# Layer 1's first eight blocks of edge records, loaded by SyncE during the node stage

## The reference

```
# layer 0: per edge a tensor product of x[dst] with 32 edge attributes, summed by src
tp = fctp_messages(x[dst], edge_attr_32, W1, W2, W3, W4)
agg = segment_sum(tp @ Wm + bm, src)
x = layernorm(x + x + concat(x, agg) @ Wu + bu)
# layer 1: per edge a radial weight from 10 lengths, times y[src] and 4 edge attributes, summed by dst
w = relu(edge_attr_10 @ W_fc1 / sqrt(10)) * sqrt(2) @ W_fc2 / sqrt(100)
y = linear(x) * a            # W_l1_0, W_l1_1
s = segment_sum(products of w, y[src], edge_attr_4, dst) / 4
x = layernorm(x + self(x) * a + 0.5 * linear(s) * a)
```

## Time and profile before

| | |
|---|---|
| median of three runs | 2830.84 us |
| the profiled execution's own time | 2835.33 us |
| its span | 2833.5 us |
| TensorE busy (matmul) | 2614.8 us, 92% |
| VectorE | 1979.4 us, 70% |
| ScalarE | 852.2 us, 30% |
| GpSimd | 1662.2 us, 59% |
| granted TensorE clock, mean | 0.977 |

### The profile page before, as it was taken

One profiled execution on the slowest core, in us unless ns is written; L12 is line 12 of the kernel. 1 busy time (PEld: TensorE's weight loads), 2 busy tenths in 40 slices (PEclk: granted clock), 3 DMA queues, 4 the chain that ended last, 5 costly groups with the idle time before them and its releaser, 6 DMA issues. The chain is left out here.

```text
span 2833.5 us, 54044 instructions
## 1 busy us (share of the span) xinstructions
PE 2614.8 (92%) x16778; PEld 2330.6 (82%) x16778; DVE 1979.4 (70%) x5259; ACT 852.2 (30%) x2319; POOL 1662.2 (59%) x1770
## 2 busy tenths in 40 slices
PE   4999999999999999996999968999999999998997
PEld 2888788888888888886999958988888888888886
DVE  7677567766667767663777856766777676667766
ACT  2444344444444444431222212222222222222221
POOL 1666566666666666662100017777777777777775
PEclk8999999999999999998999979999999999999999
DMA  6899999999888999865888845333333333333332
GB/s 232 294 314 314 299 319 316 319 324 320 290 290 287 291 300 294 294 215 187 279 279 280 284 141 149 90 86 88 100 86 90 86 101 88 86 88 99 87 88 68
DMA packets 433880, 584.01 MB, mean 206 GB/s; under 512 B 75752, under 2 KB 372409, under 8 KB 421002
## 3 DMA queue, kind: packets, MB, share of 16 engines
q10 hardware_dynamic: 237795, 282.85, 30.4%
q0 software_dynamic: 84144, 149.09, 17.9%
q1 hardware_dynamic: 111656, 148.48, 16.3%
HBM read 352.08 MB, written 228.11 MB: 205 GB/s over the span
## 5 line engine op out<-in xcount | busy, mean ns | idle before, releaser
L444 POOL DMA_INDIRECT placed<-message,slots_now x784 | 762.9, 973 | 486.5 <-ACT message L613 326.6
L1429 POOL DMA_INDIRECT f_y<-y_table,b_rec x894 | 855.4, 957 | 289.6 <-issue 181.9
L528 PEld LDWEIGHTS g_bank<-quad_ring,front_work 128*128 128x128 f32 x6272 | 878.5, 191 | 98.9 <-issue 96.5
L528 PE MATMUL g_bank<-quad_ring,front_work 128*128 x6272 | 942.1, 304 | 8.0 <-DMA quad_ring<-products 7.5
L772 DVE SCALAR_TENSOR_TENSOR front_work<-g_bank,quarter_node,front_work 128x512 f32<-128x512 f32 x784 | 529.6, 743 | 44.2 <-PE g_bank L505 31.8
L1619 PE MATMUL e_bank<-f_msg,f_hot 128*126 128x160 f32 x1788 | 387.6, 312 | 71.7 <-DVE f_msg L1493 70.6
L1490 DVE TENSOR_TENSOR f_msg<-e_bank,f_y 128x256 f32<-128x256 f32 x447 | 189.2, 423 | 319.7 <-issue 223.9
L1614 PE MATMUL e_bank<-f_msg,f_hot 128*126 128x160 f32 x1788 | 395.8, 303 | 18.0 <-DVE f_msg L1493 15.3
L1619 PEld LDWEIGHTS e_bank<-f_msg,f_hot 128*126 128x126 f32 x1788 | 282.0, 189 | 122.9 <-DVE f_msg L1493 121.4
L1602 PE MATMUL e_bank<-fc,b_hidden 100*128 100x192 f32 x1788 | 372.0, 330 | 0.0
L613 ACT COPY message<-g_bank 128x320 f32<-128x320 f32 x392 | 167.2, 427 | 561.9 <-PE g_bank L528 561.9
(11 more groups left out here) (237 smaller groups left out, 2622.7 us busy)
## 6 DMA issues: line engine op xcount, KB each, us to landing
products<-g ACTq DMA_DIRECT2D x49, 2560.0 KB
quad_ring<-products ACTq DMA_DIRECT2D x98, 1280.0 KB
big<-placed SPq DMA_DIRECT2D x49, 1458.0 KB, 7.1
front_work<-in_e_t SPq DMA_DIRECT2D x392, 64.0 KB
b_lengths<-length_parts ACTq DMA_DIRECT2D x447, 45.0 KB
placed<-zeros SPq DMA_DIRECT2D x24, 648.0 KB
f_y<-y_table,b_rec POOLq DMA_INDIRECT x894
placed<-message,slots_now POOLq DMA_INDIRECT x784
```

The lines of the kernel that those rows point to most:

```text
L444: pool.indirect_dma_start(v.placed[:, :], bass.IndirectOffsetOnAxis(slots_now[tile // SET % SLOT_SETS][:, tile % SET:tile % SET + 1], 0), ...
L528: last = pe.matmul(bank_now[:, n * D:n * D + D], spread[batch % SPREADS][:, j, q * P:q * P + P], ring[:, bass.ds(slot + j, 1), :].rearrang ...
L1429: pool.indirect_dma_start(f_y[:, tile % Y_RING, :], None, v.y_table[:, :], bass.IndirectOffsetOnAxis(b_rec[b % REC_RING][:, j, 0:1], 0)).t ...
```

## The change

The tiles `b_rec` are allocated before the node stage and live on. In the fast form of the node stage, SyncE's list gets a fifth entry, last in each step: at steps 24 to 31 it loads the register and issues the records of one of the first eight blocks. One semaphore, `first_records`, counts all eight. In layer 1 these loads are gone; GpSimd and VectorE wait for `first_records` at block 0 and for the tile's own semaphore from block 8 on. The semaphore `excess_ready` is gone: what it counted is counted on `misfit_ready`, and TensorE waits for 2 there.

```diff
+        v.b_rec = [sb(f"b_rec{q}", [P, TPB, 6], I32) for q in range(REC_RING)]
+        v.first_records = sem("first_records")
...
-                pe.wait_ge(excess_ready, 1)
-                pe.wait_ge(misfit_ready, 1)
+                pe.wait_ge(misfit_ready, 2)
...
+        RECORDS_FROM = 24
...
-                (unrolled if fast else skewed)(sp, FAST_BLOCKS, N, (7 if fast else 4, load_rows), (5 if fast else 4, load), (1, store), (0, landed))
+                def load_records(b):
+                    first = sp.value_load(v.block_start[b:b + 1, :], min_val=0, max_val=TILES * P)
+                    edges = t["records"][bass.ds(first, BLOCK_EDGES), :]
+                    sp.dma_start(v.b_rec[b][:].rearrange("p j a -> p (j a)"), edges.rearrange("(p j) a -> p (j a)", p=P)).then_inc(v.first_records, 16)
+
+                def some_records(i, k):
+                    b = i * N + k - RECORDS_FROM
+                    if 0 <= b < REC_RING:
+                        load_records(b)
...
+                unrolled(sp, FAST_BLOCKS, N, (7, load_rows), (5, load), (1, store), (0, landed), (0, some_records))
...
-                    if b >= REC_RING:
-                        sp.wait_ge(weighed, (b - REC_RING + 1) * BPP)
+                    sp.wait_ge(weighed, (b - REC_RING + 1) * BPP)
...
-                for b in range(REC_RING):
-                    load_block(b // SUBS, b % SUBS)
...
-                        pool.wait_ge(rec_in[b % REC_RING], 16 * (b // REC_RING) + 16)
+                        if b == 0:
+                            pool.wait_ge(v.first_records, 16 * REC_RING)
+                        if b >= REC_RING:
+                            pool.wait_ge(rec_in[b % REC_RING], 16 * (b // REC_RING))
```

More of the change, by code:

```diff
@@ L44 @@
 SLOTS = ROWS * P
+REC_RING = 8
 LEAST = 14 * P
@@ L283, in front_phase @@
         tiles_counted, nodes_in, start_ready = sem("tiles_counted"), sem("nodes_in"), sem("start_ready")
-        excess_ready, misfit_ready, held_summed, violations_summed = sem("excess_ready"), sem("misfit_ready"), sem("held_summed"), sem("violations_summed")
+        misfit_ready, held_summed, violations_summed = sem("misfit_ready"), sem("held_summed"), sem("violations_summed")
         features_doubled = sem("features_doubled")
@@ L692, in block_starts @@
                     tables.link(dve.tensor_tensor(excess[:], starts[:, 2:4], starts[:, 0:2], ALU.subtract))
-                    dve.tensor_scalar(excess[:], excess[:], float(BLOCK_EDGES), 0.0, ALU.subtract, ALU.max).then_inc(excess_ready, 1)
+                    dve.tensor_scalar(excess[:], excess[:], float(BLOCK_EDGES), 0.0, ALU.subtract, ALU.max).then_inc(misfit_ready, 1)
                 def weights():
@@ L946, in landed @@
                     sp.sem_inc(stored, 1)
-                (unrolled if fast else skewed)(sp, FAST_BLOCKS, N, (7 if fast else 4, load_rows), (5 if fast else 4, load), (1, store), (0, landed))
+                def load_records(b):
[6 more added lines that the diff above has]
+                        load_records(b)
+                if not fast:
+                    for b in range(REC_RING):
+                        load_records(b)
+                    skewed(sp, FAST_BLOCKS, N, (4, load_rows), (4, load), (1, store), (0, landed))
+                    return
+                unrolled(sp, FAST_BLOCKS, N, (7, load_rows), (5, load), (1, store), (0, landed), (0, some_records))
             def fast_sync(sp):
@@ L1286, in layer1_edges @@
         HIDDEN_RING = 3
-        REC_RING = 8
         COLUMNS = 4
-        b_rec = [v.sb(f"b_rec{q}", [P, TPB, 6], I32, local) for q in range(REC_RING)]
+        b_rec = v.b_rec
         b_column = [v.sb(f"b_column{q}", [P, TPB], F32, local) for q in range(COLUMNS)]
@@ L1465, in localise @@
                 def localise(b):
-                    dve.wait_ge(rec_in[b % REC_RING], 16 * (b // REC_RING) + 16)
+                    if b == 0:
+                        dve.wait_ge(v.first_records, 16 * REC_RING)
+                    if b >= REC_RING:
+                        dve.wait_ge(rec_in[b % REC_RING], 16 * (b // REC_RING))
                     dve.tensor_scalar(b_column[b % COLUMNS][:], b_rec[b % REC_RING][:, :, 1], v.block_base[:, b:b + 1], None, ALU.subtract).then_inc(columns, 1)
```

## The result

The changed kernel takes 2837.04 us (median of 17 runs, 2831.18 to 2843.23) against 2830.84 for the kernel before (17 runs, 2824.16 to 2836.99): ratio 1.0022, 95% interval 1.0014 to 1.003. In a second comparison it was 1.0013 (1.0004 to 1.0022). It is slower by about 0.2%, and the predicted 2834.8 was 2.2 us too low.

What follows compares the result with a forecast made beforehand. POOL's gathers bound layer 1; PE and a loop through SP, level, bound the node stage. Node stage +3.6 and layer 1 +0.4 gave +4.0 us, a median of 2834.8 against 2830.84; range 2829.0 to 2840.0.

Steps and rivals of the forecast that it cites:

- The bound: Layer 1 bound by POOL's gathers; node stage by PE and a loop through SP, level, so added delay has no cover.
- (a): Node stage, steps 24 to 31: each record load delays SP's placed rows by 1.45 us; stage +3.6 us.
- 0.8 of 2.0 us of unevenness: Node stage: 2.0 us of the eight steps measured before was unevenness; a longer loop keeps less than half, adding 0.8.
- The landing on an emptier queue: Node stage: placed rows issued later land sooner, in 6.85 us instead of the median 7.1.
- The register load: Node stage: SP's register load from DRAM stays near the quiet figure, 0.45 to 0.66 us, between two placed-row loads.
- (b): Layer 1 opening: POOL can gather 2.6 us earlier, but only about 1.1 is free before it waits for pair 8's weighing.
- (c): Layer 1 opening: own-table copy starts eleven us earlier beside ACT's first loads; pair 8 weighed 1.6 us later, layer +0.4.
- The upper bound of +2.6: Layer 1: worst case if ACT's register loads cost 2.25 us and nothing is regained; 4.7 - 1.1 = 3.6, rounded down.
- A: Node stage: SP's register loads slow, 1.2 us more each; +8.4 there and +0.4, 2839.6 us; chance 0.16.
- B: Node stage: the queue, not the issue, is the limit; stage pays 0.2, POOL keeps 1.1 to 2.6; 2829.2 us; chance 0.15.
- C: Layer 1 opening: loads beside the copy cost 2.6, plus node stage 3.6; +6.2, 2837.0 us; chance 0.10.
- D: Layer 1: POOL is not released earlier because it is late itself; worth 0 on top of the forecast; chance 0.04.

Runs made afterwards that it cites:

- second comparison: The changed kernel, unaltered, run again on another chip against the kernel before: 2843.57 us, ratio 1.0013.
- the reordering: Changed kernel with the eight record loads moved ahead of SyncE's wait for the finished block: 2837.97 us, 0.9994 of the kernel before; 0.9985 on a slower chip.
- the dose: Two thrown-away register loads a step in 32 node-stage steps, added to Copy at 1: 2854.0 us (1.0063) behind the store, 2838.69 (1.0013) ahead of the wait.
- Copy at 1: The reordering, plus layer 1's copy of the own table held until one pair is weighed: 2835.01 us (0.998 of the kernel before); other chips 0.9986 and 1.0.
- at 7: The reordering, plus layer 1's copy of the own table held until seven pairs are weighed: 2837.74 us, 0.9991 of the kernel before; 0.9984 on a slower chip.
- the version at the tail: Copy at 1 with records behind the store at steps 42 to 45, two blocks each, after the last placed-rows load: 2831.84 us, 0.9989 of the kernel before.

## Why the prediction was right or wrong

**The bound.** Right. Layer 1's end follows the gathers: from pair 16's gather to the last one it is 1086.13 us before and 1084.91 after. The node stage has no cover for SP's delay, as the reordering (5.6 us in the whole time for nothing but a place, 2.7 of them in the node stage of the profiles) and the dose (16.3 us in the node stage) show.

**(a) The node stage: mechanism right, size within what single profiles tell.** Forecast +3.6 for eight steps. The first pair of profiles gives +5.5, the second, changed against reordered, +3.0. The pieces: the placed rows left 2.22 to 3.08 us after the store, 1.3 us later than before on average where I took 1.45 (the mean before was 1.2, not 0.95); they landed in 6.6, where I took 6.85. Both were a shade too dear. Neither pair of profiles can size the rest, for which I kept 0.8 of 2.0 us of unevenness. Steps of 7 and of 8 to 9 us stand side by side in every kernel, also in the one before, where the one from block 25's store to block 26's takes 9.39, just outside the eight. With two more steps (stores of blocks 25 to 35) the first pair differs by 8.3 us and the second by 1.0. The dose is the better measure, as it runs over 32 steps: an estimate from it, eight loads at 1.3 us of delay of which a third arrives, is 3.3 us. So the forecast's +3.6 may well be right, and whether a record load makes the steps more uneven is not shown.

**The landing on an emptier queue.** Right in direction, and the dose gives its size: of 1.6 us more delay 0.5 is given back by the shorter landing, and a third reaches the step where a loop over two steps would pass on half.

**The register load.** Right for the changed kernel: 0.457 us. The Trainium skill (DMA: Bandwidth & Descriptors, Latency and other measured facts) gives such a load a floor of about 600 ns and an access to HBM 2 us at high load. The traces go below the floor on SP (0.457 us) and agree with the 2 us: in the reordered kernel, where the same instruction starts 3 us or more ahead of the store, it took 2.26.

**(b) and (c), the opening.** Right in the main pieces. First gather 2.2 us earlier after the last store (2.6 forecast); waits in front of pairs 15 and 16, as said; pair 16 gathered 0.26 us later after the last store (+0.4 forecast). ACT's first register loads cost 2.0 instead of 1.8. Copy at 1 and at 7 show that the copy is the cause of the waits, which the prediction had only argued. The upper bound of +2.6 doesn't follow from its own sum, which gives 3.6 and is "rounded down"; the second comparison, +1.4, stays inside either.

**The rivals.** A (slow register loads in the node stage) falls: 0.636 at most in the first profile, and 1.043 once in the second. B (the queue was the limit) falls: 5.5 and 3.0 us in the profiles, not 0.2, and 16.3 in the dose. C's number, 2837.0, is the measured 2837.04, but by luck: its mechanism falls in the first comparison, where the opening lost 0.26, not 2.6. In the second the waits were longer (4.0 us against 2.4) and pair 16 came 1.4 us later than before after the last store, halfway to C. D falls: POOL was released earlier.

**The sum.** +4.0 forecast, +6.2 measured at first (by the interval 4.0 to 8.5) and +4.8 in the second comparison (1.1 to 6.2). The forecast lies inside the second interval and at the edge of the first. Where the remaining 1 or 2 us are is not known: the profile of the changed kernel is only 2.4 us above the one before. The loss sat just over the border of 0.2%, an outcome that I had given 0.27.

**Open.** Why pair 8 is weighed between 45.0 and 48.9 us, and the first gather starts between 7.65 and 8.53 us, after the last store in kernels with one and the same opening; why the version at the tail gains more than copy at 1; and the 2.7 us by which the stages ahead differ between two profiles, which I take for scatter but didn't test.

## What to carry to other kernels

Before work is put into an engine's idle time, ask what stands behind it in that engine's list: the kernel with the same eight record loads was 5.6 us slower with them behind the store than ahead of the wait, and they cost nothing measurable at the end, where no loop depends on them. When a prefetch leaves the head of a stage, the bulk transfer that it stood in front of starts earlier too, and can slow the loads that now run beside it; a wait in front of that transfer took the slowing away here, though the whole time didn't show the gain reliably. And where two bounds are level, a delay in one loop is neither hidden nor passed on whole: a dose over many steps gives the fraction, here a third, and more surely than the profile of eight steps, whose scatter was as large as the effect.

## What the runs showed of the hardware

The same register load from DRAM took 0.44 to 0.48 us on SP (medians of three profiles) in the gap between two bulk transfers, and a median of 2.26 (up to 2.71) while one was in flight; on ACT 0.63 to 0.74 quiet and 1.7 to 2.2 beside the copy. Loads of 1458 KB issued 1.6 us later in the step landed in 6.5 us against 7.0 (medians of 33 and 34). On one of the three chips of the experiments the same kernel took 13% longer (3193.94 against 2838.77 and 2835.78 on the others), most of it in layer 1, and the reordered kernel's granted clock was 0.926 there against 0.976; no run here tells why.
